# Between two attentions: the kept part of the update moves from ScalarE and GpSimd to VectorE

## The reference, cut to what matters

```
x_diff = x[:, None, :, :] - select_mean_diff[None, :, None, :]
x_diff = x_diff / jnp.linalg.norm(x_diff, axis=3, keepdims=True)
cont = jnp.einsum('nds,bntd->bnts', select_weight, x_diff) ** 2
score = cont.sum(axis=-1)
gate = jax.nn.sigmoid(imp_slope * (score - imp_center))
sel_scale = gate.max(axis=1)[..., None]
sel_idx = gate.argmax(axis=1)
...
return (1.0 - sel_scale) * x + sel_scale * mod_x_bias
```

## Time and profile before

| what | value |
|---|---|
| median of three runs | 692.51 us (691.39 to 693.83) |
| the profiled execution: its time | 691.39 us |
| the profiled execution: its span | 689.6 us |
| VectorE busy, share of the span | 454.7 us, 66% |
| TensorE busy (matmul) | 565.9 us, 82% |
| ScalarE busy | 351.8 us, 51% |
| GpSimd busy | 246.0 us, 36% |
| first and last normalization L927 | 208.2 and 267.6 us |
| kept updates L936 | 16 of 585 ns, 230.2 to 260.7 us |

### The profile page before, as it was taken

How to read it: one execution, slowest core, us unless ns; L and a number is a source line. 1 busy time by engine, 2 the same in 40 slices (tenths; PEclk the granted TensorE clock), 3 DMA queues, 4 the chain that set the end, 5 groups by cost and what they waited for, 6 DMA issues and landing times.

```text
span 689.6 us, 14424 instructions
## 1 busy us (share of the span) xinstructions
PE 565.9 (82%) x4178; PEld 399.6 (58%) x4179; DVE 454.7 (66%) x1327; ACT 351.8 (51%) x890; POOL 246.0 (36%) x343
## 2 busy tenths in 40 slices
PE   4997779899879699888778797745568999989985
PEld 2564445466458654556556565523456787768774
DVE  4557658588337874666696773654758777767764
ACT  1542347477745677256645556422014566556663
POOL 2432000010503215355334353447503555545540
PEclk9997699899999999999979999977659999999999
DMA  7587955700000005956105152144233444444488
GB/s 235 191 269 238 259 149 159 214 4 2 3 1 1 2 0 175 283 177 213 52 2 202 55 181 84 49 182 161 86 93 109 147 146 153 138 136 147 147 335 341
DMA packets 49535, 95.20 MB, mean 138 GB/s; under 512 B 8580, under 2 KB 40524, under 8 KB 46924
## 3 DMA queue, kind: packets, MB, share of 16 engines
q1 hardware_dynamic: 41804, 75.34, 35.2%
q0 software_dynamic: 7680, 19.21, 7.4%
HBM read 58.54 MB, written 35.59 MB: 136 GB/s over the span
## 4 chain that ended last, share of the span: by engine, by line
PE 43%; DVE 23%; DMA 10%; issue 8%; ACT 6%; POOL 4%; SPq 3%; another core or an unknown queue 2%; DVEq 0%; POOLq 0%; ACTq 0%
PE banks L1524 6%; PE banks L1318 6%; PE banks L1151 4%; PE banks L1274 4%; DMA arena<-negT 4%; PE banks L1339 3%; PE banks L1535 3%; DVE mx L1827 3%; POOL results_by_rank L875 3%; PE banks L1157 2%; DVE mx L1830 2%; DMA parts_dram<-arena 2%; DMA arena<-results_by_rank 2%; PE banks L1433 2%
## 5 line engine op out<-in xcount | busy, mean ns | idle before, releaser
L1019 ACT ACTIVATE arena<-banks 128x512 f32<-128x512 f32 (+1 forms) x256 | 130.4, 548 | 100.5 <-PE banks L1318 69.6
L1318 PE MATMUL banks<-arena 98*128 98x256 bf16 (+1 forms) x512 | 90.7, 273 | 37.3 <-DMA arena<-negT 13.8
L875 POOL DMA_INDIRECT results_by_rank<-attn_w,goes x80 | 77.1, 963 | 90.0 <-issue 70.6
L1827 DVE TENSOR_REDUCE mx<-banks 128x4 f32<-128x1024 f32 x64 | 76.1, 1220 | 29.9 <-PE banks L1274 29.9
L1274 PE MATMUL banks<-arena 96*128 96x256 bf16 (+1 forms) x512 | 90.5, 284 | 4.5 <-DVE mx L1827 2.6
L1318 PEld LDWEIGHTS banks<-arena 98*128 98x128 bf16 x512 | 43.9, 102 | 72.4 <-ACT arena L1019 16.3
L1524 PE MATMUL banks<-arena,attn_w 128*128 x320 | 84.8, 388 | 0.5 <-issue 0.4
L840 POOL DMA_INDIRECT rows_by_expert<-arena,bpb x64 | 62.9, 983 | 52.6 <-ACT arena L1019 30.9
L1830 DVE TENSOR_REDUCE mx<-banks 128x4 f32<-128x1024 f32 (+1 forms) x48 | 57.9, 1221 | 27.1 <-PE banks L1278 26.9
L1274 PEld LDWEIGHTS banks<-arena 96*128 96x128 bf16 x512 | 53.4, 106 | 22.8 <-DVE mx L1827 6.8
L1524 PEld LDWEIGHTS banks<-arena,attn_w 128*128 128x128 f32 x320 | 55.8, 195 | 5.8 <-issue 1.2
(11 more groups left out here) (243 smaller groups left out, 1105.9 us busy)
## 6 DMA issues: line engine op xcount, KB each, us to landing
arena<-parts_dram SPq DMA_DIRECT2D x72, 256.0 KB, 4.6
pvs<-rows_by_expert SPq DMA_DIRECT2D x80, 130.0 KB
parts_dram<-arena SPq DMA_DIRECT2D x24, 384.0 KB, 3.5
arena<-results_by_rank SPq DMA_DIRECT2D x6, 1024.0 KB, 10.1
arena<-in SPq DMA_DIRECT2D x2, 2304.0 KB
rows_by_expert<-zero SPq DMA_DIRECT2D x1, 4160.0 KB, 23.6
arena<-in SPq DMA_DIRECT2D x2, 1920.0 KB
arena<-in SPq DMA_DIRECT2D x3, 768.0 KB
```

What stands on the lines that cost most here:

```text
L875: pool.indirect_dma_start(ys, bass.IndirectOffsetOnAxis(ap=goes[:, j:j + 1], axis=0), yb[j], None).then_inc(y_stored[j], 16)
L1019: act.activation(p_ring[n][:, i % P_RING, :], st_bank[RING_AT[n]["s", b, s] % 3][:, 0:P_WIDTH[n]], ACT.Exp, scale=HD ** -0.5).then_inc(exp ...
L1318: ins = pe.matmul(dst[:, at:at + SEQ - q0], keys, q_rows(n, slice(0, ROWS), s, b, q0, SEQ - q0), start=True, stop=(n == 0 or b < POOL_MASKS))
L1827: ins = dve.tensor_reduce(out, src.rearrange("p (q h k) -> p q h k", q=QT, k=nk), AX.X, ALU.max)
```

## The change

The sum of squares `xx` is no longer worked out on GpSimd from the variance. ScalarE squares the normalized rows of a chunk with a row sum, one operation a tile (`squares`, in the order's stage C, the end of the tick), into a buffer that nothing reads (`junk`, which is the second buffer of F's normalized rows).

The kept update is no longer an operation on x on ScalarE with scale and shift from GpSimd. VectorE does it as the last part of `gate`, as x = normalized row * keep + x, one operation a tile. So B(3) of ScalarE now waits for the first kept update, since VectorE reads the rows of B for longer.

ScalarE's exponential is issued after all normalizations of the tick, and reads values that VectorE has clamped at -80 in one more step; before, VectorE clamped the exponential's result inside a step that was there anyway.

```
--- before.py
+++ after.py
@@ scalar: normalize, squares, gate_exp @@
-            def normalize(stage, c, dst, ready, gated):
+            def normalize(stage, c, dst, ready):
                 act.wait_ge(norm_ready, NORM_STAGES.index((stage, c)) + 1)
+                if dst is xn2[1] and c == 1:
+                    act.wait_ge(squares_ready, TILES)
                 if ready is xn1_ready and c >= 3:
-                    act.wait_ge(job_ready[1], JOBS1.index((c - 3, "TC1")) + 1)
+                    act.wait_ge(kept, c - 2)
                 for t in range(CT):
...
-                    if t == 1 and gated is not None:
-                        gate_exp(gated)
-
-            def add_kept(c):
-
-                act.wait_ge(keep_scaled, c + 1)
-                for n in range(c * CT, (c + 1) * CT):
-                    ins = act.activation(x[:, n, :], x[:, n, :], ACT.Identity, bias=row_shift[:, n:n + 1],
-                                         scale=row_scale[:, n:n + 1])
-                ins.then_inc(kept, 1)
+            def squares(c):
+                for t in range(CT):
+                    act.wait_ge(xn1_ready, c * CT + t + 1)
+                    if c:
+                        act.wait_ge(squares_ready, (c - 1) * CT + t + 1)
+                    act.activation(junk[:, t, :], xn1[c % 3][:, t, :], ACT.Square,
+                                   accum_out=xx[c % 2][:, t:t + 1]).then_inc(squares_ready, 1)
...
-                act.activation(sc[c % 2][1][:, :, :], sc[c % 2][3][:, :, :], ACT.Exp, scale=-1.0
+                act.activation(sc[c % 2][1][:, :, :], sc[c % 2][0][:, :, :], ACT.Exp, scale=-1.0
...
-                for stage, c in wave(tick, "FBHE"):
+                for stage, c in wave(tick, "FBHDC"):
...
+                    elif stage == "D":
+                        gate_exp(c)
                     else:
-                        add_kept(c)
+                        squares(c)
@@ vector: gate @@
-                dve.wait_ge(squares_ready, c + 1)
+                dve.wait_ge(squares_ready, (c + 1) * CT)
...
-                dve.tensor_tensor(s3, s2, col(slob), ALU.mult).then_inc(logit_ready, 1)
+                step(1, dve.tensor_tensor(s3, s2, col(slob), ALU.mult))
+
+                dve.tensor_scalar(s0, s3, -80.0, None, ALU.max).then_inc(logit_ready, 1)
                 dve.wait_ge(gate_exp_ready, c + 1)
-                step(1, dve.tensor_scalar(s2, s1, FINITE, 1.0, ALU.min, ALU.add))
+                step(1, dve.tensor_scalar(s2, s1, 1.0, None, ALU.add))
...
+                for t in range(CT):
+                    rows = x[:, c * CT + t, :]
+                    ins = dve.scalar_tensor_tensor(out=rows, in0=xn1[c % 3][:, t, :], scalar=keep[p][:, t:t + 1], in1=rows,
+                                                   op0=ALU.mult, op1=ALU.add)
+                ins.then_inc(kept, 1)
@@ gpsimd: scale, scale_kept @@
-                if stage == "B":
-                    then(pool.tensor_tensor(xx[:, at], rstd[:, at], rstd[:, at], ALU.mult))
-                    then(pool.tensor_tensor(xx[:, at], xx[:, at], mv[:, at, 1], ALU.mult))
-                    pool.tensor_tensor(xx[:, at], xx[:, at], width[:, :], ALU.mult).then_inc(squares_ready, 1)
-
-            def scale_kept(c):
-
-                at = slice(c * CT, (c + 1) * CT)
-                pool.wait_ge(keep_found, c + 1)
-                pool.wait_ge(norm_ready, NORM_STAGES.index(("B", c)) + 1)
-                then(pool.tensor_tensor(row_scale[:, at], keep[c % 2][:, :], rstd[:, at], ALU.mult))
-                pool.tensor_tensor(row_shift[:, at], keep[c % 2][:, :], shift[:, at], ALU.mult)
-                pool.tensor_tensor(row_scale[:, at], row_scale[:, at], ones[:, 0:CT], ALU.add).then_inc(keep_scaled, 1)
```

More of the change, by code:

```diff
@@ L303, in two_block_kernel @@
                      for at, size in ((0, FW), (CT * FW, NSEL * SELW), (CT * (FW + NSEL * SELW), MW)))
[L304 to L306 removed]
+        xx, top, least, keep = ([sb(f"{name}{i}", [P, CT]) for i in range(2)] for name in ("xx", "top", "least", "keep"))
         sc = [[sb(f"sc{n}_{i}", [P, CT, NSEL]) for i in range(4)] for n in range(2)]
@@ L381, in two_block_kernel @@
         mid_done = sem("mid_done")
+        pool_norm = sem("pool_norm")
         norm_ready = sem("norm_ready")
@@ L810, in _ @@
             for tick in range(TICKS):
-                for stage, c in wave(tick, "FBHD"):
+                for stage, c in wave(tick, "FBH"):
                     if stage == "H":
                         low(c)
-                    elif stage == "D":
-                        scale_kept(c)
                     else:
@@ L1048, in _ @@
                             turn_copy(c, f"T{stage}{k}", turned["ACG".index(stage)][:, k, :])
-                gated = dict(wave(tick, "D")).get("D")
-                last_norm = [stage for stage, c in wave(tick, "FB")][-1:]
-                for stage, c in wave(tick, "FBHE"):
+                for stage, c in wave(tick, "FBHDC"):
                     if stage == "F":
-                        normalize("F", c, xn2[c % 2], xn2_ready, gated if last_norm == ["F"] else None)
+                        normalize("F", c, xn2[c % 2], xn2_ready)
                     elif stage == "B":
-                        normalize("B", c, xn1[c % 3], xn1_ready, gated)
+                        normalize("B", c, xn1[c % 3], xn1_ready)
                     elif stage == "H":
                         middle(c)
+                    elif stage == "D":
+                        gate_exp(c)
                     else:
-                        add_kept(c)
+                        squares(c)
             wait_saved(act, 1, range(len(SPLIT1)))
@@ L1681, in gate @@
                 dve.wait_ge(mid_done, done_upto(JOBS1.index((c, "SL1"))))
-                dve.wait_ge(squares_ready, c + 1)
-                dve.scalar_tensor_tensor(out=s2, in0=g[p][:, :, a:a + NSEL], scalar=-2.0,
-                                         in1=row(xx[:, c * CT:(c + 1) * CT]), op0=ALU.mult, op1=ALU.add)
+                dve.wait_ge(squares_ready, (c + 1) * CT)
+                dve.scalar_tensor_tensor(out=s2, in0=g[p][:, :, a:a + NSEL], scalar=-2.0, in1=row(xx[p]),
+                                         op0=ALU.mult, op1=ALU.add)
                 step(1, dve.tensor_tensor(sq[p], g[p][:, :, 0:a], g[p][:, :, 0:a], ALU.mult))
```

22 lines of the change are left out of this document (9 added, 13 removed).

## The result

The kernel after the change takes 700.39 us (median of 8 runs, 698.62 to 703.19) against 693.17 us before (8 runs beside them, 690.41 to 697.74). The ratio is 1.0117, 95% interval 1.0090 to 1.0145. By the ratio it is slower by 8.1 us; these two medians alone are 7.2 apart. Over all 27 timed runs of the kernel after the median is 701.09 us. The forecast was 700.5 us, 8.0 us more than before.

A forecast was written before the change was run, and what follows sets the result against it. VectorE's chain was taken to bound ticks 4 to 6 of the stage between the attentions: 0.15 + 3.04 + 6.34 - 1.53 = 8.0 us, added to 692.51, gives 700.5 us; 8 in 10 for 697.5 to 704.0.

The forecast's parts named there:

- Kept operations on VectorE: VectorE, ticks 3 to 6: four added operations per chunk, 1.58 us each chunk, 6.34 us in all before F(2).
- The wait for the kept update: VectorE at the start of ticks 5, 6 and 7: three waits of 0.51 us for ScalarE go, 1.53 us back.
- The exponential: ScalarE, ticks 3 to 6: issued behind all four normalizations, it delays VectorE by 0.76 us a tick, 3.04 us.
- The clamp: VectorE's added step in each gate: 0.23 us, hidden behind ScalarE; without that cover 0.9 us in all.
- The squares: ScalarE, end of ticks 2 to 5: 0.50 us each; only tick 2's push the next tick, by 0.15 us.
- Rival 4: ScalarE: square and exponential share no function table, so loads add 6.4 us, 706.9 us; chance 7%.
- The 4.54 us wait: VectorE in tick 8, ahead of F(3), for ScalarE's kept update: off the path, so its removal gives nothing back.
- From F(2) on: After tick 7: H(0), `low(0)`, SyncE's chain and the start of attention 1 all move by 8.0 us with F(2).
- TensorE: At DN(3)'s second half it waits some 3 us instead of 0.77 for H(0)'s bank, so projections move by 8.0.
- rival 3: TensorE's clock falls behind the new 3 us wait at DN(3), adding 1.3 us, 701.8 us; chance 20%.

The follow-up runs named there:

- e1: Kernel before with only the kept update moved to VectorE at the end of the gate; ratio 1.0060.
- e9: Kernel before with ScalarE's kept update ahead of the normalizations, plus 22 and 18 idle TensorE turns ahead of TM(1) and TM(2); ratio 0.9947.
- e2: Kernel before with only ScalarE's exponential moved behind all four normalizations, kept update still on ScalarE; time that of before within its interval.
- e6: Kernel after with the exponential back behind the second normalized tile and without the added clamp step; ratio 1.0059.
- e7: Kernel after with fifteen small dependent VectorE operations ahead of F(3)'s adds, holding it back 7.6 us; ratio 1.0087.
- e11: Kernel before, unchanged, executed once more for a second profile; 689.12 us.
- e8: Kernel after with 32 idle turns of a constant on TensorE ahead of each of TM(1) and TM(2); ratio 1.0114.
- e12: Kernel after, unchanged, executed once more for a second profile; 702.58 us.
- e10: Kernel before with only 22 and 18 idle turns on TensorE ahead of TM(1) and TM(2); ratio 0.9954.
- e4: Kernel before with ScalarE's kept update issued ahead of the tick's normalizations; time not shorter, stage 92.10 us against 90.98.
- e5: Kernel after with the exponential put back behind the tick's second normalized tile, clamp step kept; ratio 1.0092.

## Why the prediction was right

Its terms against what they measured, in its own order:

- *Kept operations on VectorE*, 6.34 us forecast: 4 x 1.58 measured. e1 has it alone. The Trainium skill's rule on it (Vector Engine (DVE) Microarchitecture Reference, "Points that are easy to get wrong") would have given an estimated 4 us more and is not borne out: four in 1.66 us.
- *The wait for the kept update*, 1.53 us forecast to come back: some 1.8 (6.34 less the 4.60 of e1 is 1.74, and e9 has 1.78). A wait that is seen as 0.51 us also stops the next operation from starting some 0.09 us before the last one ends (236.12 in the kernel after, where the last of the kept operations ends at 236.20), so it is worth 0.60. This and the squares' 0.15 are why F(2) moved by 7.58 and not by 8.0 us.
- *The exponential*, 3.04 us forecast: 3.63 - 2.89 = 0.74 in each tick, 3.0. e2 shows what the prediction didn't say, that it is worth only 1.2 without the first part. *The clamp* was hidden, and shown by e6 to be worth 0.87 otherwise.
- *The squares*, 0.15 us forecast: 0. They take 0.40 us each, not 0.50. Rival 4 falls, there are no loads. The Trainium skill (ScalarE: Activation LUTs, "Table sets: the hidden batching unit") says that cheap functions are in every set and doesn't name the square; this trace has the square in the set that also serves the exponential, and shows nothing of the other sets.
- *The 4.54 us wait* was off the path (e7). F(3) starts right behind H(0), and `low(1)` moved by 6.63 us (6.7 forecast).
- *From F(2) on*: `low(0)` moved by 7.59 us, 56.04 to 63.63 after the first add, as forecast with F(2).
- *TensorE* is the step that went otherwise. The prediction had it move at DN(3), behind a wait of 3 us. In the profile after there is no wait there. The waits ahead of TM(1) and TM(2) were 4.5 and 4.4 us (6 and 4 were named), but behind the second the clock fell and made TensorE late by itself: project(1) moved by 8.01 us, 0.4 more than VectorE would have made it. In the second profile the wait at DN(3) was there (1.59 us) with the clock's fall behind it, as rival 3 had it, and project(1) took 2 us more. The stage so took 7.25 us more in one profile and 9.45 in the other, where VectorE's path alone gives 7.6 (against e11, the other profile of the kernel before, it is 6.3 and 8.5). The 7.25 are TensorE's 8.0, less the 0.4 that its path had in hand before (rival 3 names them: 278.92 and 279.36 us), less 0.3 that the first issues of the second stack took less.

So the mechanism on VectorE was right, and the median lay as near to the forecast as it did partly by luck. Two small errors went against each other: F(2) was put 0.4 us too far, and the clock's fall, held for a rival at 20%, is in every profile of that schedule. Each of the four profiles with the kept update on VectorE and the exponential late (after, e7, e8, e12) has a fall behind TM(2) or DN(3) that lengthens TensorE's work by 1.7 to 4.5 us, partly hidden. At rival 3's own place, DN(3), it is in e8 and e12. How often it is there in the timed runs is not known; their median over all 27, 701.09 us, lies between the forecast and rival 3's 701.8.

What stays open: filled waits made the kernel before 0.46% faster (3.2 us of the median, interval 1.2 to 5.1), and its profile doesn't show where; its stage is as long as before. The mean granted clock of the whole span, which is listed for every run, has its median at 0.924 in e10 and 0.925 in e9 against 0.917 in the kernel before beside them. As the lower level is half of the upper, I estimate from these that TensorE was at the lower one for some 10 us less. Where in the program those lie, and whether they or the place of the falls make the 3.2 us, was not shown.

## What to carry to other kernels

Work may be moved from an engine with slack to the one whose chain sets the pace only if the wait that goes is larger than the work that comes, and the wait must be read from the stage: of the four waits for the kept update, three worth 0.60 us each were on the path and the largest, of 4.5 us, was not. Two edits that share a cover don't add up: the late exponential costs 1.2 us under the kept update's wait and 3.0 without it. Where an engine waits often and its clock may fall behind a wait, follow its path as a second one to the end, since it can take the place of the first.

## What the runs showed of the hardware

- An activation with a row sum is two instructions, the activation (128x256 f32, 403 ns) and a read of the accumulator (190 ns), but they overlap: 0.40 us from one square to the next. The normalizations of the same size, with two pointer operands, take 585 ns and start 0.50 us apart.
- Square, exponential, copy and identity alternate in this stage without a table load (12 loads in the program, all elsewhere, as before).
- scalar_tensor_tensor of 128x256 f32 from two SBUF sources with a pointer scalar: four in 1.66 us, 0.40 us apart.
- Behind one and the same wait TensorE's granted clock fell to 0.50 in some executions and not in others (2.88 us ahead of TM(1) in the kernel before: a fall in the first profile, none in e11; 2.49 us ahead of TM(2): a fall in e4, none in the first profile of before). Behind a wait of 1.59 us at DN(3) it fell in e1, e5, e8 and e12 (in e1, e8 and e12 with a shorter wait just before), behind 1.42 us there in e6 and 1.83 us ahead of TM(2) in e10 it did not. Filling a wait with idle turns kept the clock at that place, and in e8 it fell at the next.
- The landing of the last save took 4.0 us (e11) to 6.1 us (e6) between executions.
